# A pipeline of slots for a cosine stage, a loop written out, and norms begun a stage early

## The reference, cut to what matters

```python
x = x + tanh(g_xattn[i]) * cross_attention_i(layernorm(x), ctx)   # i = 0..3
x = x + tanh(g_ffn[i])   * feed_forward_i(layernorm(x))           # i = 0..3, in turn
```

```python
v = layernorm(x) @ Wv.T + bv            # (32, 128, 64)
t = ctx @ Wt.T + bt                     # (32, 128, 64)
cosine[s, t] = dot(v[s], t[t]) / max(norm(v[s]) * norm(t[t]), 1e-8)
x = x + tanh(g) * cosine                # 128 x 128 per sequence
```

## Time and profile before

| | |
|---|---|
| median of 3 runs | 2226.41 us (2219.57 to 2226.76) |
| profiled execution | 2225.49 us |
| its span, first to last instruction | 2223.7 us |
| executed instructions | 47787 |
| mean granted TensorE clock | 0.933 |

### The profile page before, as it was taken

The page is one execution under the profiler, slowest core; times in us unless marked ns, Lnnn a source line. Parts: engine busy times, 40 slices in busy tenths (PEclk is TensorE's granted clock), DMA queues, the critical chain, the costliest instruction groups (busy, mean ns, idle before and its releaser), DMA issues. The chain is left out here.

```text
span 2223.7 us, 47787 instructions
## 1 busy us (share of the span) xinstructions
PE 1990.5 (90%) x18071; PEld 1505.1 (68%) x18071; DVE 1573.9 (71%) x3176; ACT 1244.3 (56%) x2822; POOL 794.1 (36%) x692
## 2 busy tenths in 40 slices
PE   6668999999998799969999996897998799999986
PEld 3358999899987466646666664675585566666666
DVE  5789999999998888844444535765476666666665
ACT  3269888888882567742332323784522466666641
POOL 1034454444554233305444544432000233333333
PEclk7579999999999899989999998998999899999995
DMA  2100000000000200016335430001000000000001
GB/s 61 44 1 8 9 15 8 14 14 9 14 8 3 81 9 9 2 31 141 77 84 124 101 78 18 11 1 54 1 1 8 5 5 5 5 5 5 1 1 40
DMA packets 41407, 61.71 MB, mean 28 GB/s; under 512 B 9464, under 2 KB 18208, under 8 KB 40800
## 3 DMA queue, kind: packets, MB, share of 16 engines
q1 hardware_dynamic: 41184, 58.66, 10.8%
HBM read 56.02 MB, written 2.62 MB: 26 GB/s over the span
## 5 line engine op out<-in xcount | busy, mean ns | idle before, releaser
L842 POOL TENSOR_TENSOR a_probs<-a_probs,a_rsums 128x1024 f32<-128x1024 f32 x64 | 121.3, 1896 | 317.7 <-DVE a_rsums L892 317.7
L1545 POOL TENSOR_TENSOR f_h<-f_gated,f_w_spread 128x512 f32<-128x512 f32 x128 | 161.4, 1266 | 196.0 <-DVE f_gated L1599 89.3
L1599 DVE TENSOR_TENSOR f_gated<-f_silu,f_up 128x512 f32<-128x512 f32 x128 | 87.0, 685 | 183.9 <-PE f_up L1676 172.6
L1639 ACT ACTIVATE f_silu<-f_gate 128x512 f32<-128x512 f32 x128 | 76.4, 597 | 232.8 <-PE f_gate L1676 231.9
L2375 ACT ACTIVATE f_combine<-f_logits,f_neg_row_max 128x128 f32<-128x128 f32 x512 | 198.5, 395 | 0.5 <-DVE f_neg_row_max L2233 0.5
L2194 POOL TENSOR_TENSOR f_slot_sum<-f_slot_sum,f_logits 128x512 f32<-128x512 f32 x96 | 122.7, 1279 | 180.0 <-DVE f_slot_max L2312 94.7
L1691 PEld LDWEIGHTS f_acc<-f_down,f_h 128*128 128x128 f32 x1024 | 129.8, 193 | 42.9 <-issue 38.0
L2202 POOL TENSOR_TENSOR f_acc<-f_acc,f_row_factor 128x512 f32<-128x512 f32 x128 | 136.8, 1070 | 60.7 <-DVE f_slot_max L2312 38.5
L2436 PE MATMUL f_give_bank<-f_y,f_combineT 128*128 128x128 f32 x1024 | 141.0, 281 | 12.8 <-DVE f_y L2282 7.5
L880 DVE TENSOR_REDUCE a_negmax<-a_score_bank 128x8 f32<-128x1024 f32 x64 | 78.3, 1223 | 101.6 <-PE a_score_bank L1026 101.6
L2425 PE MATMUL f_slot_bank<-f_logits,f_xn 128*128 128x128 f32 x1024 | 136.8, 277 | 6.5 <-issue 5.5
(11 more groups left out here) (331 smaller groups left out, 4968.4 us busy)
## 6 DMA issues: line engine op xcount, KB each, us to landing
f_w_spread<-f_routing_rows SPq DMA_DIRECT2D x64, 512.0 KB, 9.4
f_w<-in_f_w SPq DMA_DIRECT2D x16, 256.0 KB, 2.5
a_cT<-in_ctxT SPq DMA_DIRECT2D x16, 192.0 KB, 2.5
f_gate_up<-in_f_guT SPq DMA_DIRECT2D x1, 2048.0 KB, 7.3
out<-x_resident SPq DMA_DIRECT2D x8, 256.0 KB, 2.4
c_cT<-in_ctxT SPq DMA_DIRECT2D x8, 192.0 KB, 2.8
a_ctx<-in_ctx SPq DMA_DIRECT2D x8, 192.0 KB, 2.6
f_phi<-in_f_phi SPq DMA_DIRECT2D x1, 1024.0 KB, 6.3
```

The lines of the kernel that those rows point to most:

```text
L842: nc.gpsimd.tensor_tensor(probs[:, u], probs[:, u], rsums[:, u, :].unsqueeze(2).to_broadcast([S, 8, S]), ALU.mult).then_inc(normalised, 1)
L1545: nc.gpsimd.tensor_tensor(h[:, u % KEPT, :], gated[:, u % 2, :], w_spread[:, u // PER, u % PER, :], ALU.mult).then_inc(weighted, 1)
```

## The change

Layer 0 becomes a pipeline over slots -3 to 8 with at most one group in each place: in slot t VectorE normalises group t+2, takes the statistics of t+3, rescales t-1, keeps the lengths of t and adds the cosines of t-1; the copy of the turned rows is the first thing that ScalarE does in a slot. The projections are laid out on both halves of the array (sequences of a group in pairs: `half(r)`), so the emptying has 128 rows and 256 columns. Both squared lengths come from one-column matmuls, their power of -1/2 is taken on GpSimd, and the text length is spread over the columns by a diagonal matrix and a matmul by ones; the limit 1e-8 on the product of the norms becomes a limit 1e8 on the product of the inverses. Context tiles go ahead of the weights, over four buffers instead of two.

The loop of layer 1 is written out as 154 steps. Layer 4's tail computes the norm of the first two groups for layer 5, and layer 5's walk computes it for layer 6. At the start of layer 4 the two first context tiles are loaded ahead of the small vectors, the clearing of `neg` moves to slot -3 and the wait for the bias to slot 0. The diff, with repeated parts left out:

```diff
@@ layer0_cosine @@
...
+                for g in range(GROUPS):
+                    if g == 2:
+                        load(sp, weights, loads)
+                    if g >= 4:
+                        sp.wait_ge(projected, g - 3)
+                    sp.dma_start(cT[:, g % 4, :], ctx_groups[:, g, :]).then_inc(ctx_landed[g % 4], 16)
+                for t in SLOTS:
+                    if there(t + 3):
+                        norm.gpsimd_rstd(pool, *at(t + 3))
+                    if there(t):
+                        s = t % 2
+                        pool.wait_ge(lengths_kept, t + 1)
+                        if t >= 2:
+                            pool.wait_ge(scale_done, t - 1)
+                        nc.gpsimd.tensor_tensor(inverse[:, s].rearrange("p k j -> p (k j)"),
+                                                lengths[:, s].rearrange("p k j -> p (k j)"), core.minus_half[:, 0:2 * G],
+                                                ALU.pow).then_inc(inverted, 1)
+                        pool.wait_ge(inverted, t + 1)
+                        if t >= 2:
+                            pool.wait_ge(spread, t - 1)
+                        nc.gpsimd.tensor_tensor(diagonal[:, s], core.ident[:, :].unsqueeze(1).to_broadcast([S, G, S]),
+                                                inverse[:, s, 1].unsqueeze(2).to_broadcast([S, G, S]),
+                                                ALU.mult).then_inc(diagonal_done, 1)
+                def keep_lengths(g):
+                    dve.wait_ge(summed, g + 1)
+                    if g >= 2:
+                        dve.wait_ge(inverted, g - 1)
+                    nc.vector.tensor_scalar(lengths[:, g % 2].rearrange("p k (m r) -> p k m r", r=2),
+                                            length_bank[:, :].rearrange("p (r n) -> p r n", r=2)[:, :, 0:4]
+                                            .rearrange("p r (k m) -> p k m r", k=2), SMALLEST, None,
+                                            ALU.max).then_inc(lengths_kept, 1)
+                def rescale(g):
+                    dve.wait_ge(spread, g + 1)
+                    for j in range(G):
+                        last = nc.vector.tensor_scalar(scale[:, j, :], spread_bank[:, j * S:(j + 1) * S],
+                                                       inverse[:, g % 2, 0, j:j + 1], 1.0 / EPS, ALU.mult, ALU.min)
+                    last.then_inc(scale_done, 1)
+                def add_cosines(g):
+                    x = core.X_groups[:, g // 2, g % 2]
+                    dve.wait_ge(dotted, g + 1)
+                    dve.wait_ge(scale_done, g + 1)
+                    nc.vector.tensor_tensor(cosine[:, :, :].rearrange("p (m r) n -> p r m n", r=2),
+                                            dot_bank[:, :].rearrange("p (r n) -> p r n", r=2)[:, :, 0:2 * S]
+                                            .rearrange("p r (m n) -> p r m n", m=2),
+                                            scale[:, :, :].rearrange("p (m r) n -> p r m n", r=2),
+                                            ALU.mult).then_inc(cosine_done, 1)
+                    dve.wait_ge(cosine_done, g + 1)
+                    nc.vector.scalar_tensor_tensor(out=x, in0=cosine[:, :, :], scalar=core.gates[:, 0:1], in1=x,
+                                                   op0=ALU.mult, op1=ALU.add).then_inc(updated, 1)
+                for t in SLOTS:
+                    if there(t + 2):
+                        if t + 2 >= 2:
+                            dve.wait_ge(norm.turned, t + 1)
+                        norm.vector_normalise(dve, *at(t + 2))
+                    if there(t + 3):
+                        if t + 3 == 2:
+                            dve.wait_ge(core.x_landed[1], 16)
+                        norm.vector_stats(dve, *at(t + 3))
+                    if there(t - 1):
+                        rescale(t - 1)
+                    if there(t):
+                        keep_lengths(t)
+                    if there(t - 1):
+                        add_cosines(t - 1)
+                act.wait_ge(weights, LOADED)
+                def empty(g):
+                    s = g % 2
+                    act.wait_ge(projected, g + 1)
+                    if g >= 2:
+                        act.wait_ge(summed, g - 1)
+                        act.wait_ge(dotted, g - 1)
+                    for out, ps, bias, func in ((v2, v_bank, bvc, ACT.Square), (t2, t_bank, btc, ACT.Square),
+                                                (vT, v_bank, bvc, ACT.Identity), (tT, t_bank, btc, ACT.Identity)):
+                        last = nc.scalar.activation(out[:, s].rearrange("p k n -> p (k n)"), ps[:, 0:2 * S], func,
+                                                    bias=bias[:, 0:1])
+                for t in SLOTS:
+                    if there(t + 2):
+                        g = t + 2
+                        act.wait_ge(norm.turned, g + 1)
+                        if g >= 2:
+                            act.wait_ge(projected, g - 1)
+                        nc.scalar.activation(norm.xT[:, g % 2, :], turn_bank[:, :], ACT.Copy).then_inc(norm.xT_ready, 1)
+                    if there(t + 1):
+                        empty(t + 1)
+                def project(g):
+                    pe.wait_ge(ctx_landed[g % 4], g // 4 * 16 + 16)
+                    pe.wait_ge(norm.xT_ready, g + 1)
+                    if g:
+                        pe.wait_ge(squared, g)
+                    for r in range(2):
+                        nc.tensor.matmul(t_bank[half(r), 0:2 * S].rearrange("p (k n) -> p k n", k=2), wt[:, :],
+                                         of_half(cT[:, g % 4, :], r), start=True, stop=True)
+                    for r in range(2):
+                        last = nc.tensor.matmul(v_bank[half(r), 0:2 * S].rearrange("p (k n) -> p k n", k=2), wv[:, :],
+                                                of_half(norm.xT[:, g % 2, :], r), start=True, stop=True)
+                    last.then_inc(projected, 1)
+                def sum_squares(g):
+                    s = g % 2
+                    pe.wait_ge(squared, g + 1)
+                    if g:
+                        pe.wait_ge(lengths_kept, g)
+                    for what, squares in enumerate((v2, t2)):
+                        for k in range(2):
+                            for r in range(2):
+                                first = 512 * r + 2 * what + k
+                                last = nc.tensor.matmul(length_bank[:, first:first + 1], squares[half(r), s, k, :],
+                                                        core.ones[half(r), 0:1], start=True, stop=True)
+                    last.then_inc(summed, 1)
+                def products(g):
+                    s = g % 2
+                    if g:
+                        pe.wait_ge(cosine_done, g)
+                    for k in range(2):
+                        for r in range(2):
+                            first = 512 * r + k * S
+                            last = nc.tensor.matmul(dot_bank[:, first:first + S], vT[half(r), s, k, :], tT[half(r), s, k, :],
+                                                    start=True, stop=True)
+                    last.then_inc(dotted, 1)
+                def spread_inverse(g):
+                    pe.wait_ge(diagonal_done, g + 1)
+                    if g:
+                        pe.wait_ge(scale_done, g)
+                    nc.tensor.matmul(spread_bank[:, :], core.ones[:, :], diagonal[:, g % 2].rearrange("p j n -> p (j n)"),
+                                     start=True, stop=True).then_inc(spread, 1)
+                for t in SLOTS:
+                    if there(t - 1):
+                        products(t - 1)
+                    if there(t + 2):
+                        if t + 2:
+                            pe.wait_ge(norm.xT_ready, t + 2)
+                        norm.tensor_turn(pe, *at(t + 2))
+                    if there(t - 1):
+                        spread_inverse(t - 1)
+                    if there(t):
+                        sum_squares(t)
+                    if there(t + 1):
+                        if t + 1 == 0:
+                            pe.wait_ge(weights, LOADED)
+                        project(t + 1)
...
@@ layer6_attention, gpsimd and vector @@
                 pool.sem_inc(normalised, 2)
-                for at in (FIRST, SECOND):
-                    norm.gpsimd_rstd(pool, *at)
...
                 dve.sem_inc(updated, 1)
-                norm.vector(dve, *FIRST)
-                norm.vector(dve, *SECOND)
                 dve.wait_ge(held.landed, held.all)
@@ layer5_experts @@
             def _(pool):
-                for g in range(GROUPS):
+                for g in range(2, GROUPS):
                     norm.gpsimd_rstd(pool, *at(g))
+                for g in range(2):
+                    next_norm.gpsimd_rstd(pool, *at(g))
...
             def _(dve):
-                norm.vector_stats(dve, *at(0))
-                norm.vector_stats(dve, *at(1))
```

(39 more changed lines are left out.)

141 lines of the change are left out of this document (33 added, 108 removed).

## The result

The changed kernel takes **2187.75 us** (median of 4 runs, 2180.97 to 2191.7), the kernel before 2225.32 beside it: a ratio of 0.9828, 95% interval 0.981 to 0.9846. I had forecast 2183 with a range of 2170 to 2198. The saving is 37.6 us by the medians; my sum was 42.8.

A forecast was written before the change was run, and what follows sets the result against it. Stages end at barriers; a chain round the engines bounds the cosine stage, VectorE the soft mixture. Savings 29 + 8.3 + 1.1 + 1.5 + 2.9 = 42.8 us off 2225.49 gave 2182.7, forecast as 2183, range 2170 to 2198.

The forecast's parts named there:

- my sum: Whole kernel: savings of cosine stage, written-out loop and three joints added up to 42.8 us.
- What bounds: Whole kernel: barriers separate the stages; a chain round the engines bounds the cosine stage, VectorE the soft mixture.
- The cosine stage: Layer 0: mostly full clock, slots of 7.2 and 5.7 us, end at 74.8, 29 us saved, bounds 15 and 38.
- my best bound of 66.4: Cosine stage: its end in us if every slot took 5.6, which would save 38.
- Rival A: Cosine stage: clock stays at 0.5 to 0.66, only 15 to 20 us saved there, 2195 in all; chance 0.17.
- Rival B: Cosine stage: diagonal doesn't hold up the normalise, slots near 5.6, 38 us saved, 2171 in all; chance 0.17.
- The loop: Soft mixture written out: 5.4 us from GpSimd's register waits and 3.15 from jumps, taken as 8.3, bounds 3 and 10.
- Rival C: Soft mixture: writing out the loop gives only its jumps, 2188 us in all; chance 0.10.
- Rival D: Soft mixture: written-out code comes late and TensorE stalls, making the kernel slower, about 2230 us; chance 0.02.
- Joint 3 to 4: Layer 4's start: the clearing stops the first normalise but frees VectorE earlier, 1.1 us saved, bounds 0 and 3.4.
- Joint 4 to 5: Layer 5's start: early normalises free the first transpose, the second waits for w1; 1.5 us saved, bounds 0 and 2.4.
- Joint 5 to 6: Layer 6's start: first projection 3.3 us earlier, waiting for the context tile; 2.9 saved, bounds -1.3 and 3.3.

The follow-up runs named there:

- e1: The kernel before with the new cosine stage alone, its soft mixture loop as before: 2212.17 us, ratio 0.9946.
- g2: The changed kernel with matmuls of the identity filling TensorE's idle time throughout the cosine stage: 2179.83 us, ratio 0.9783.
- g1: The changed kernel with the cosine stage's diagonal made by ScalarE instead of GpSimd: 2196.43 us, ratio 0.987.
- e2: The kernel before with the soft mixture's loop written out and nothing else: 2217.02 us, ratio 0.997.
- e4: The changed kernel with GpSimd's stream of the soft mixture alone put back into the loop: 2191.43 us, ratio 0.9849.

## Why the prediction was right, and where its sum was off

- **What bounds.** Right in kind: a loop between the engines decided the cosine stage, and barriers kept the stages apart, with one exception that I did not see (e1): behind another stage the same loop stood twice at each jump.
- **The cosine stage, mis-sized by 5.5 us: the share of half clock.** The step that failed is "I take mostly full clock with dips: 7.2 for the five slots that hold a transpose, 5.7 for two." The first five measured 36.7 together against my 36.0, because slots of 6.15 stood beside slots of 8.13 (my 6.8 and 9.1 were both too high, in part because the diagonal takes 1.04, not 1.3). The last two measured 6.97 each at half clock, 2.5 more than my sum. First lengths came at 22.31 and not 20.4: transposes, projections and sums at half pace, and four emptyings of 0.36 each. The tail took 7.9 instead of 7.0. Together 1.9 + 0.7 + 2.5 + 0.9 = 6.0 at the last update (80.8 against 74.8). g2 shows the cause: with the clock held up, the stage ends at 68.0, close to my best bound of 66.4. Full clock was 13.7 us of 78, the reverse of "mostly"; that the stage came as near as 5.5 us is in part luck, since a slot at half clock was 1.0 cheaper than I had priced it. My reason was the wrong row: the window from 160 to 180 us in the earlier trace rows has a like busy share, but a like share did not bring a like clock. And the 0.66 beside it, which I read as the stage's clock, was 0.58.
- **Rival A** had the clock right and the price wrong: the mean was 0.59, inside its 0.5 to 0.66, but slots at half clock took 8.1 and 7.0 us, not 9.1 and 7.6, so that the 23.5 saved lie between its 15 to 20 and the 29.
- **Rival B** is out: 1.84 to 1.86 us beside the diagonal, 1.11 without it (g1), and 3.55 beside the clearing. By the Trainium skill ("SBUF — State Buffer", Who interferes with whom) the port pair goes to one of the two for a whole instruction; all three agree. The power of the earlier trace rows doesn't: 2.91 us long, it left the four tiles beside it at their usual 1.11.
- **The loop**: 7.88 against 8.3 (8.65 in e2, alone), but the two terms were mis-sized against each other, so the near hit is in part luck. GpSimd's looped stream costs 614.89 - 608.22 = 6.7 us (e4), with its own jumps, against my 5.4. About 1.2 are left for the jumps of the others, by difference, against 3.15; and 2.0 of those 3.15 are the one chunk in which the clock fell. **Rival C** is out. **Rival D** too: chunks of 34.3 us, and 2.39 + 0.62 MB of instructions for 47,251, 64 bytes each again. What I missed is that in this company the loop was worth 15.8 (e1, one execution), so the kernel before with the new stage and its old loop would have been a poor bargain.
- **Joint 3 to 4**: x's normalise at 9.62 us after the layer's first statistics instead of 10.85, 1.2 against 1.1, and VectorE freed by the end of the clearing as worked out.
- **Joint 4 to 5**: second transposes 4.62 us after the barrier's first operation instead of 6.37, 1.75 against 1.5, and waiting for w1. Layer 5 gained 3.7: the clock rose sooner (the first hidden matmuls 4.90 against 5.47 us). e1, without the joint, took 154.86, so I don't count the rest as the joint's.
- **Joint 5 to 6**: the projection 2.75 us after the first issue instead of 6.16, and 3.0 for the layer against 2.9.
- **What my sum did not have** is layer 4's end: in the profiled execution TensorE's clock fell 173 us into the layer, and 180 us into it in g1 with the same code. By the layer's length that is 189.63 - 183.98 = 5.7 us, and hides the joint there. Layers 2, 3 and 7 moved by -1.8, 0.9 and 1.8 with no edit; the 34.0 of this execution against the 37.6 of the medians lies within that.

## What to carry to other kernels

In a stage that is a ring of short operations, price each slot at both clocks and ask which of the two its idle time will bring; a busy share borrowed from another stage doesn't tell. A written-out loop is worth its register waits and its jumps, and the jumps have no fixed price: count the stalls at each and look whether the clock falls behind them, in more than one execution. Ahead of the first record of the clock read the level from the pace of a known matmul, not from the column. Filling TensorE's idle time pays where the fill ends before the operand comes, so price it by the very instruction that does it.
